# Feed-forward inputs prepared during the attention, and every second tile's gelu turned by a transfer

## The chip, the cores and the metric

The kernel runs on one core of one Trainium2 chip. The metric is the device time in microseconds, as the median of three runs. TensorE (PE) does the matmuls, VectorE (DVE), ScalarE (ACT) and GpSimd (POOL) the work on elements; SyncE (SP) issues nearly all transfers. SBUF is the memory on chip with 128 partitions, PSUM the banks into which TensorE writes, HBM the memory outside.

## The reference

One transformer layer on X of shape (32, 256, 128): `X = X + attention(norm(X))` with 16 heads of size 64, and then `X = X + ffn(norm(X))`. For each token the feed-forward part is

```
h = norm(norm(x)) * g1 + lb1            # 128 numbers
h = gelu(h @ T1 + b1)                   # T1: ternary weights, 128 x 512
h = norm(h) * g2 + lb2                  # 512 numbers
out = h @ T2 + b2                       # T2: ternary weights, 512 x 128
```

There are 8192 tokens, that is 64 tiles of 128 tokens. Nearly float32 precision is wanted, so each operand of a matmul is split in two 16-bit numbers, a high part and the low rest, and a product is three matmuls: high x high, high x low, low x high.

## The kernel before

The program of each engine is written out by hand as a loop over the same steps; semaphores order the engines. `attention_steps` yields pairs (t, u). A step t handles pair t of heads (256 pairs, 8 to a batch of 256 tokens, so t = 8 b + j); from step 80 to 239 two steps are done as one ("paired", `two_steps`). A turn u handles the feed-forward part: in turn u each engine does its piece of tile u minus a lag. Turns 0 to 23 lie beside steps 245 to 268, later turns stand alone. X lies in SBUF throughout, the attention adds its output to it, and `ffn_root` leaves `r1` and `nm1`, the scale and shift of the second norm, for each batch.

Attention, as far as it is touched: TensorE computes queries and keys (`queries_keys`, bank QK), scores for the maxima (`max_scores`, bank M) and scores (bank S, in paired steps also the pair of banks named misc); ScalarE takes the exponentials (`exps`, L1000) and the high halves (QKh L1008, xp L962, O L1023), GpSimd the low halves of p (`p_low`, L1210), of x (`x_low`, L1195) and of the outputs (L1216). `x_norm` (L955) normalises two batches ahead. SP turns x, the shifts and the outputs by transposing transfers.

Feed-forward, tile i of 128 tokens, in four-tile groups g:

- turn i: ScalarE normalises the tile, `f_y` (L1107). After four tiles, y is split (ScalarE and VectorE for the first three groups, then GpSimd: `f_ysplit`, L1292 and L1294), and SP turns the group with one transfer, `turn_y`.
- turn i + 10: TensorE's `f_hidden` (L853 to L855, three matmuls of 512 columns into half of M), ScalarE's gelu into a ring of four f32 tiles a (L1115).
- turn i + 11: TensorE's `f_zT` turns a with four f32 transposes into half of S (L864); ScalarE rounds this to zTh (L1121); VectorE takes the statistics of a (L1600, L1607) and the low part zTl (L1613).
- turn i + 13: TensorE's `f_out`, twelve matmuls (L878 to L880).
- turn i + 14: GpSimd adds the bias to X (L1299). Once per group `f_root` gets the scales (L1281, L1283, L1287).
- turn i + 17: VectorE adds the scaled output to X (L1621), and SP stores four tiles at a time.

gelu's argument is scaled by `s_f1` and the turned copy by `inv_f1`, its reciprocal; the sum is scaled by `s_f12`.

Of the kernel before, what the change touches and what calls it, by code (L numbers as in the profile page):

```python
# [13 lines left out]
P = 128  # L14
# [24 lines left out]
L_BIAS, L_HID, L_ZT, L_OUT, L_SUM = 14, 10, 11, 13, 17  # L39
Y_EARLY = 3  # L40
# [28 lines left out]
    "s_f1", "inv_f1", "s_f12", "T2_less", "bias2"))}  # L69
# [86 lines left out]

def split_groups(b, j):
# [80 lines left out]

def misc_bank_no(kind, key):

    return 0 if kind in ("y", "qk") or kind in ("turn", "spread") and key in ("qk", "pg") else 1
# [8 lines left out]
def layer(nc, x_in, wq_in, wk_in, wv_in, wp_in, bp_in, g1_in, lb1_in, w1_in, b1_in,  # L250
          g2_in, lb2_in, w2_in, b2_in, out):
    with ExitStack() as ctx:
# [26 lines left out]
        inv_f1, s_f12 = sb("inv_f1", [P, 1]), sb("s_f12", [P, 1])  # L279
# [22 lines left out]


# [25 lines left out]
        y = [sb(f"y{i}", [P, FG, D]) for i in range(2)]  # L329
        yp = [sb(f"yp{i}", [P, FG, 2, D], F16) for i in range(2)]  # L330
        yT = [sb(f"yT{i}", [P, FG, 2, P], F16) for i in range(2)]
        a = [sb(f"a{i}", [P, F]) for i in range(A_RING)]
        zTh = [sb(f"zTh{i}", [P, FC, P], F16) for i in range(3)]
        zTl = [sb(f"zTl{i}", [P, FC, P], F16) for i in range(3)]
        st2 = [sb(f"st2_{i}", [P, 6]) for i in range(2)]
# [13 lines left out]
        yt_in = [sem(f"s_ffn_y_transposed{i}") for i in range(2)]  # L349
# [26 lines left out]
        s_zt, s_zhi, s_zlo = (sem(f"s_ffn_{n}") for n in ("zT", "zT_hi", "zT_lo"))  # L376
        s_xb, s_f, s_out = sem("s_ffn_x_plus_bias"), sem("s_ffn_out"), sem("s_ffn_sum")
# [57 lines left out]
        def p_high(r):  # L435

            words = p32[r][:, :, :, :].rearrange("p i m n -> p (i m n)").bitcast(BF16)
            return words.rearrange("p (i m n two) -> p i m n two", i=2, m=NB, two=2)[:, :, :, :, 1]

# [53 lines left out]
        def sp_program(e):  # L493
# [40 lines left out]
            def turn_y(g):  # L534
                e.wait_ge(s_ylo, g + 1)
                if g >= 2:
                    e.wait_ge(s_pre, FG * (g - 1))
                e.dma_start_transpose(yT[g % 2][:, :, :, :].rearrange("p k s n -> p (k s) n"),
                                      yp[g % 2][:, :, :, :].rearrange("p k s d -> p (k s d)")).then_inc(yt_in[g % 2], 16)
# [13 lines left out]
            for t, u in attention_steps():  # L553
# [10 lines left out]
                if u == FG + 1:  # L564
                    turn_y(0)
                if u is not None and u % FG == 0 and FG < u <= NT:
                    turn_y(u // FG - 1)
# [8 lines left out]
        def pe_program(e):  # L576
# [267 lines left out]
            def f_hidden(i):  # L844
                g, k = divmod(i, FG)
                if k == 0:
                    e.wait_ge(yt_in[g % 2], 16 * (g // 2 + 1))
# [9 lines left out]
            def f_zT(i):  # L857
                e.wait_ge(s_a, i + 1)
                if i == 0:
                    e.wait_ge(s_ex, NP)  # L860
                if i >= 2:
                    e.wait_ge(s_zlo, i - 1)
                for c in range(FC):
                    op = e.transpose(z_bank[i % 2][:, c * P:(c + 1) * P], a[i % A_RING][:, c * P:(c + 1) * P], ident[:, :])  # L864
                op.then_inc(s_zt, 1)

            def f_out(i):
                g, k = divmod(i, FG)
                e.wait_ge(s_zlo, i + 1)
                if i == 0:  # L870
                    e.wait_ge(s_qklo, NP)
                elif i == FG:
                    e.wait_ge(s_o, NP)
                elif k == 0:
                    e.wait_ge(s_out, FG * (g - 1))
                o = f_bank(i)[:, k * D:(k + 1) * D]
                for c in range(FC):
                    e.matmul(o, zTh[i % 3][:, c, :], T2h[:, c, :], start=c == 0, stop=False)  # L878
                    e.matmul(o, zTh[i % 3][:, c, :], T2l[:, c, :], start=False, stop=False)
                    op = e.matmul(o, zTl[i % 3][:, c, :], T2h[:, c, :], start=False, stop=c == FC - 1)  # L880
                op.then_inc(s_f, 1)

            def f_out_last(i):
                e.wait_ge(s_zhi, i + 1)
                e.wait_ge(s_x1, B)
                o = last_out
                for c in range(FC):
                    e.matmul(o, zTh[i % 3][:, c, :], T2h[:, c, :], start=c == 0, stop=False)
                    e.matmul(o, zTh[i % 3][:, c, :], T2l[:, c, :], start=False, stop=False)
                e.wait_ge(s_zlo, i + 1)  # L890
                for c in range(FC):
                    op = e.matmul(o, zTl[i % 3][:, c, :], T2h[:, c, :], start=False, stop=c == FC - 1)
# [33 lines left out]
            for t, u in attention_steps():  # L926
# [9 lines left out]
                for lag, fn in ((L_HID, f_hidden), (L_ZT, f_zT)):  # L936
                    if 0 <= u - lag < NT:
                        fn(u - lag)
                if 0 <= u - L_OUT < NT - 1:
                    f_out(u - L_OUT)  # L940
                elif u - L_OUT == NT - 1:
# [4 lines left out]
        def act_program(e):  # L946
# [155 lines left out]
            def f_y(i):  # L1102
                g, k = divmod(i, FG)
                e.wait_ge(s_nm1, i // NB + 1)
                if g >= 2:
                    e.wait_ge(s_ylo, g - 1)
                e.activation(y[g % 2][:, k, 0:D - 1], X[:, i, 0:D - 1], ACT.Identity, scale=r1[:, i:i + 1],  # L1107
                             bias=nm1[:, i:i + 1]).then_inc(s_y1, 1)

            def f_gelu(i):  # L1110
                e.wait_ge(s_pre, i + 1)
                if i >= A_RING:
                    e.wait_ge(s_zt, i - A_RING + 1)
# [3 lines left out]
            def f_zhi(i):  # L1117
                e.wait_ge(s_zt, i + 1)
                if i >= 3:
                    e.wait_ge(s_f, i - 2)  # L1120
                e.activation(zTh[i % 3][:, :, :], z_bank[i % 2][:, :].rearrange("p (c n) -> p c n", c=FC),  # L1121
                             ACT.Identity, scale=inv_f1[:, :]).then_inc(s_zhi, 1)

            def f_yhi(g):
# [611 lines left out]
```

## Time and profile before

| | |
|---|---|
| median of 3 runs | 1002.25 us (1000.64 to 1003.49) |
| span of the profiled execution, first to last instruction | 998.7 us |
| own time of the profiled execution | not listed with the profile; the median stands 3.55 us above the span |
| granted clock of TensorE | 1.00 (full) in all parts |
| busy: TensorE, VectorE, GpSimd, ScalarE | 980.8, 880.0, 837.1, 729.6 us |
| chain of work that ended last | 95% on TensorE |
| transfers | 57.8 MB, mean 58 GB/s |

In a view by lines a row reads: line, engine, operation, output and inputs by their names in the program, shapes, count, then busy time and mean ns of one, then idle time before it. In a timeline the first number is the start, the second the duration, and brackets hold the idle time before, with what ended it. An instruction may start before the end of the one ahead of it on its engine, since their ends overlap; so the distance of two starts tells how long the engine is held. Transposes and matmuls have modelled ends.

### The profile page before, as it was taken

How to read it: one execution, taken by the hardware profiler on the slowest of the kernel's cores; microseconds unless marked ns; L12 is line 12 of the kernel's file. 1: busy time of each engine (PE TensorE's matmuls, PEld its weight loads, DVE VectorE, ACT ScalarE, POOL GpSimd, SP SyncE). 2: the span in 40 equal slices, each digit the busy share in tenths (PEclk: the TensorE clock that was granted, in tenths of full speed). 3: DMA queues.
4: the chain of work that ended last, by engine and by line, in shares of the span. 5: the costliest groups of instructions: out<-in, count | busy, mean ns of one | idle time of the engine just before them, and what ended most of it. 6: DMA issues, size and time to landing. Idle time of an engine off the chain costs nothing.

```text
span 998.7 us, 39391 instructions
## 1 busy us (share of the span) xinstructions
PE 980.8 (98%) x16052; PEld 782.2 (78%) x16052; DVE 880.0 (88%) x1779; ACT 729.6 (73%) x1151; POOL 837.1 (84%) x861
## 2 busy tenths in 40 slices
PE   7899999999999999999999999999999999999998
PEld 6577777778777787887887777888878777788886
DVE  7888988988889888898889988889889988788998
ACT  5687677777767777777777777777777776879995
POOL 6789888989887888888899888888888889866765
PEclk9999999999999999999999999999999999999999
DMA  6112332222331232233222233324222233354343
GB/s 141 38 32 51 53 66 45 43 49 52 74 53 27 51 73 53 52 53 71 55 48 41 48 73 51 53 53 71 46 41 47 52 52 53 69 86 75 77 86 65
DMA packets 203682, 57.82 MB, mean 58 GB/s; under 512 B 185072, under 2 KB 203248, under 8 KB 203504
## 3 DMA queue, kind: packets, MB, share of 16 engines
q1 hardware_dynamic: 201424, 54.79, 29.8%
q8 instruction: 129, 2.11, 0.9%
q10 hardware_dynamic: 2080, 0.52, 0.2%
q14 instruction: 49, 0.40, 0.1%
HBM read 7.21 MB, written 4.19 MB: 11 GB/s over the span
## 4 chain that ended last, share of the span: by engine, by line
PE 95%; DVE 2%; ACT 1%; issue 1%; POOL 1%; DVEq 0%; POOLq 0%; ACTq 0%
PE S L675 11%; PE PV L700 8%; PE M L635 7%; PE PV L702 6%; PE PV L701 6%; PE QK L622 5%; PE QK L623 5%; PE QK L624 5%; PE misc L675 5%; PE S L667 5%; PE S L864 3%; PE M L753 2%; PE M L718 2%; PE M L754 2%; PE M L755 2%; PE misc L667 2%
## 5 line engine op out<-in xcount | busy, mean ns | idle before, releaser
L1210 POOL TENSOR_TENSOR pl<-p 128x1024 f16<-128x1024 f32 x253 | 476.9, 1896 | 39.3 <-ACT p L1000 39.1
L1410 DVE TENSOR_REDUCE negmax<-M 128x4 f32<-128x1024 f32 x252 | 306.8, 1217 | 22.4 <-PE M L635 16.4
L1008 ACT ACTIVATE QKh<-QK 128x512 f16<-128x512 f32 x251 | 149.5, 596 | 155.5 <-PE QK L624 155.3
L1000 ACT ACTIVATE p<-S,s_exp 128x1024 f32<-128x1024 f32 x173 | 192.4, 1112 | 71.8 <-PE S L675 71.2
L700 PEld LDWEIGHTS PV<-V,p 128*128 128x128 bf16 x2048 | 186.8, 98 | 46.4 <-issue 34.5
L700 PE MATMUL PV<-V,p 128*128 128x65 f16 x2048 | 214.9, 194 | 4.0 <-DVE O L1424 2.9
L701 PE MATMUL PV<-V,p 128*128 128x64 f16 x2048 | 213.4, 193 | 0.0
L702 PE MATMUL PV<-V,pl 128*128 128x65 f16 x2048 | 212.6, 194 | 0.0
L1430 DVE TENSOR_TENSOR QKl<-QK,QKh 128x512 f16<-128x512 f32 x251 | 172.4, 687 | 42.2 <-ACT QKh L1008 41.1
L701 PEld LDWEIGHTS PV<-V,p 128*128 128x128 bf16 x2048 | 189.1, 97 | 4.7
L702 PEld LDWEIGHTS PV<-V,pl 128*128 128x128 f16 x2048 | 188.7, 97 | 0.0
L1216 POOL TENSOR_TENSOR O<-O,O 128x512 f16<-128x512 f32 x128 | 148.7, 1162 | 4.1 <-ACT O L1023 3.6
L622 PE MATMUL QK<-xT,Wh 128*128 128x256 f16 x502 | 136.4, 272 | 1.8 <-DVE QKl L1430 1.6
L624 PE MATMUL QK<-xT,Wl 128*128 128x256 f16 x502 | 136.8, 273 | 0.0
L623 PE MATMUL QK<-xT,Wh 128*128 128x256 f16 x502 | 136.6, 272 | 0.0
L1424 DVE TENSOR_TENSOR O<-PV,rsum 128x256 f32<-128x256 f32 x256 | 108.6, 424 | 8.8
L635 PE MATMUL M<-QKh 64*128 64x256 f16 x1016 | 98.5, 271 | 2.3 <-DVE negmax L1410 0.9
L675 PE MATMUL S<-QKh,QKl 64*128 64x256 f16 x692 | 94.5, 269 | 0.0
L675 PE MATMUL S<-QKh 64*128 64x256 f16 x692 | 94.4, 269 | 0.0
L675 PE MATMUL S<-QKl,QKh 64*128 64x256 f16 x692 | 94.4, 269 | 0.0
L1000 ACT ACTIVATE p<-misc,s_exp 128x1024 f32<-128x1024 f32 x80 | 88.7, 1109 | 0.0
L1023 ACT ACTIVATE O<-O 128x512 f16<-128x512 f32 x128 | 79.6, 622 | 0.0
(236 smaller groups left out, 2501.6 us busy)
## 6 DMA issues: line engine op xcount, KB each, us to landing
result<-X SPq DMA_DIRECT2D x15, 256.0 KB, 2.6
X<-in_L_attn_query SPq DMA_DIRECT2D x7, 512.0 KB, 4.8
OT<-O SPq DMA_TRANSPOSE x64, 4.6
shift<-negmax SPq DMA_TRANSPOSE x63, 2.3
O<-in_L_attn_Wk ACTq DMA_DIRECT2D x2, 256.0 KB, 4.3
O<-in_L_attn_Wq SPq DMA_DIRECT2D x2, 256.0 KB, 4.5
O<-in_L_attn_Wv SPq DMA_DIRECT2D x1, 512.0 KB, 3.9
w<-in_L_ffn_w SPq DMA_DIRECT2D x2, 256.0 KB, 5.6
```

Of the source, the lines that this page charges most:

```text
L622: e.matmul(o, Wh[:, i, cols], xh, start=True, stop=False)
L623: e.matmul(o, Wh[:, i, cols], xl, start=False, stop=False)
L624: op = e.matmul(o, Wl[:, i, cols], xh, start=False, stop=True)
L635: op = e.matmul(max_bank(p)[:, i * 512 + t * N:i * 512 + (t + 1) * N], h[rows, 0, t * P:(t + 1) * P], h[rows, 1, :], start=True, stop=True)
L675: op = e.matmul(bank[:, i * 512 + m * N:i * 512 + (m + 1) * N], k[rows, 1, tok], q[rows, 0, :], start=False, stop=n == 2, skip_group_check ...
L700: e.matmul(PV[:, c0:c0 + E + 1], ph[:, i, m, tok], v[:, E:2 * E + 1], start=m == 0, stop=False)
L701: e.matmul(PV[:, c0:c0 + E], ph[:, i, m, tok], v[:, 0:E], start=False, stop=False)
L702: op = e.matmul(PV[:, c0:c0 + E + 1], pl[r][:, i, m, tok], v[:, E:2 * E + 1], start=False, stop=m == NB - 1)
L1000: e.activation(p32[r][:, :, :, :].rearrange("p i m n -> p (i m n)"), score_bank(p)[:, :], ACT.Exp, scale=s_exp[:, :]).then_inc(s_ex, 1)
L1210: e.tensor_tensor(pl[r][:, :, :, :].rearrange("p i m n -> p (i m n)"), p32[r][:, :, :, :].rearrange("p i m n -> p (i m n)"), p_high(r).rea ...
L1410: e.tensor_reduce(dst[:, :, NB * jj:NB * jj + NB], max_bank(p)[:, :].rearrange("p (i t m) -> p i t m", i=2, t=NB), AX.X, ALU.max, negate=T ...
L1430: e.tensor_tensor(QKl[p % QK_RING][:, :, :].rearrange("p i n -> p (i n)"), qk_bank(p)[:, :], QKh[p % QK_RING][:, :, :].rearrange("p i n -> ...
```

## The change

1. y is prepared during the attention. `y_norm` (two normalising activations and a copy on ScalarE) of batch b - 3 stands after step 8 b + 2, `y_low` on GpSimd after 8 b + 4, `turn_y` after 8 b + 6, and `keep_y`, two steps later, writes the turned batch (128 KB) to a buffer in HBM, `y_kept`. The last batches come in turns up to 35. `f_y`, `f_yhi`, `f_ysplit`, `f_ylo` are gone; `load_y` reads a group (256 KB) back in turn 4 g + 6.
2. Tiles 0, 2, ..., 58 (30 tiles) are "in rows". They have no `f_zT`, `f_zhi` or `f_zlo`. ScalarE rounds a to bf16 as it lies (`f_zrow_high`, turn i + 10), GpSimd subtracts (`f_zrow_low`, turn i + 10), and SP turns both halves with one transfer of 256 KB (`turn_z`, turn i + 11). Their `f_out` is in turn i + 15. The other 34 tiles stay as they were, with `f_out` in turn i + 13.
3. zTh is bf16 and not scaled any more; `inv_f1` and `s_f12` are gone, the scale of the sum is `s_f2`. `f_zlo` is a plain subtraction.
4. The bias is added for four tiles at once, sums come in turn i + 18 in place of i + 17.

```
+L_BIAS, L_HID, L_ZT, L_OUT, L_OUT_ROWS, L_SUM = 13, 10, 11, 13, 15, 18
+ROWS_END = NT - 4
+Y_LAG, Y_LOW, Y_TURN, Y_KEEP = 2, 4, 6, 8
+L_LOAD = 6
+def y_batch(t, lag):
+    b, j = divmod(t - lag, HP)
+    return b - 3 if j == 0 and 0 <= b - 3 < B else None
+def in_rows(i):
+    return i % 2 == 0 and i < ROWS_END
...
+            def y_norm(b):
+                e.wait_ge(s_nm1, b + 1)
+                e.wait_ge(s_ylo, b)
+                for t in range(NB):
+                    i = NB * b + t
+                    e.activation(y[:, t, 0:D - 1], X[:, i, 0:D - 1], ACT.Identity, scale=r1[:, i:i + 1],
+                                 bias=nm1[:, i:i + 1]).then_inc(s_y1, 1)
+                e.wait_ge(s_y1, NB * b + NB)
...
+                e.activation(yp[:, :, 0, :], y[:, :, :], ACT.Copy).then_inc(s_yhi, 1)
+            def y_low(b):
+                e.wait_ge(s_yhi, b + 1)
+                e.tensor_tensor(yp[:, :, 1, :], y[:, :, :], yp[:, :, 0, :], ALU.subtract).then_inc(s_ylo, 1)
+            def turn_y(b):
+                e.wait_ge(s_ylo, b + 1)
...
+            def keep_y(b):
+                e.wait_ge(yt_in, 16 * (b + 1))
+                e.dma_start(y_kept[:, b, :], yTb[b % 2][:, :, :, :].rearrange("p t s n -> p (t s n)")).then_inc(y_kept_in, 16)
+            def load_y(g):
+                e.wait_ge(y_kept_in, 16 * (FG // NB * g + FG // NB))
                 if g >= 2:
                     e.wait_ge(s_pre, FG * (g - 1))
...
+            def f_zrow_high(i):
+                n = rows_no(i)
+                e.wait_ge(s_a, i + 1)
+                if n >= 3:
+                    e.wait_ge(zt_in[n % 3], z_turned(n - 3))
+                e.activation(z_rows_high(n), a[i % A_RING][:, :], ACT.Copy).then_inc(s_zrhi, 1)
+            def f_zrow_low(i):
+                n = rows_no(i)
+                e.wait_ge(s_zrhi, n + 1)
+                e.tensor_tensor(z_rows_low(n), a[i % A_RING][:, :], z_rows_high(n), ALU.subtract).then_inc(s_zrlo, 1)
+            def turn_z(i):
+                n = rows_no(i)
+                e.wait_ge(s_zrlo, n + 1)
+                if n >= 3:
+                    e.wait_ge(s_f, OUT_NO[i - 6])
+                e.dma_start_transpose(zT[n % 3][:, :, :, :].rearrange("p s c n -> p (s c) n"),
+                                      zp[n % 3][:, :, :, :].rearrange("p s c n -> p (s c n)")).then_inc(zt_in[n % 3], 16)
...
             def f_out(i):
                 g, k = divmod(i, FG)
...
+                if in_rows(i):
+                    n = rows_no(i)
+                    e.wait_ge(zt_in[n % 3], z_turned(n))
+                    zh, zl = zT[n % 3][:, 0, :, :].bitcast(BF16), zT[n % 3][:, 1, :, :]
+                else:
+                    n = banks_no(i)
+                    e.wait_ge(s_zlo, n + 1)
+                    zh, zl = zTh[n % 3], zTl[n % 3]
...
-                for lag, fn in ((L_HID, f_gelu), (L_ZT, f_zhi), (0, f_y)):
-                    if 0 <= u - lag < NT:
-                        fn(u - lag)
-                if u % FG == FG - 1 and u // FG < Y_EARLY:
-                    f_yhi(u // FG)
+                if 0 <= u - L_HID < NT:
+                    f_gelu(u - L_HID)
+                if 0 <= u - L_ZT < NT and not in_rows(u - L_ZT):
+                    f_zhi(u - L_ZT)
+                if 0 <= u - L_HID < NT and in_rows(u - L_HID):
+                    f_zrow_high(u - L_HID)
```

## Rows read from the trace of the kernel before

**Rows 1.** The page: busy us (share of the span) and instructions of each engine

```profile
PE 980.8 (98%) x16052; PEld 782.2 (78%) x16052; DVE 880.0 (88%) x1779; ACT 729.6 (73%) x1151; POOL 837.1 (84%) x861
```

**Rows 2.** Busy time by stretch: length, engines with counts, granted clock, transfer share, GB/s

```profile
400.00:500.00 100.00, 99.79 (x1762) 80.59 (x1758) 89.22 (x176) 70.80 (x110) 87.91 (x84) 1.00 0.30 58
...
899.00:989.70 90.70, 90.70 (x980) 73.85 (x979) 85.83 (x207) 81.27 (x146) 62.25 (x117) 1.00 0.40 74
```

**Rows 3.** Timeline of a feed-forward turn, 930 to 933 us

```profile
930.51 0.38 PE L853 MATMUL M<-T1h,yT 128*128 128x512 f16 x1
...
930.93 0.23 POOL L1281 TENSOR_SCALAR ve<-mv 128x4 f32<-128x4 f32 x1 [1.37 <-DVE mv L1607]
...
931.16 0.60 PE L864 MATMUL S<-ident,a 128*128 128x128 f32 x4
...
931.36 0.69 ACT L1115 ACTIVATE a<-M,s_f 128x512 f32<-128x512 f32 x1
...
931.59 0.22 PE L878 MATMUL QK<-T2h,zTh 128*128 128x128 f16 x1
...
931.94 0.68 ACT L1121 ACTIVATE zTh<-S,inv_f 128x512 f16<-128x512 f32 x1
...
932.26 0.38 PE L853 MATMUL M<-T1h,yT 128*128 128x512 f16 x1
...
932.38 0.30 POOL L1287 TENSOR_SCALAR rs<-r,s_f 128x4 f32<-128x4 f32 x1
...
932.66 0.75 DVE L1613 SCALAR_TENSOR_TENSOR zTl<-S,inv_f,zTh 128x512 f16<-128x512 f32 x1
```

**Rows 4.** The chain that ended last, 820 us to the end: start, us, what

```profile
873.28 1.75 DVE pl L1442
...
989.21 0.45 PE S L864 x4
```

**Rows 5.** Timeline of VectorE behind the attention, 894 to 897 us

```profile
894.51 0.68 DVE L1600 BATCH_NORM_STATS2 st<-a 128x6 f32<-128x512 f32 x1
...
895.45 0.71 DVE L1613 SCALAR_TENSOR_TENSOR zTl<-S,inv_f,zTh 128x512 f16<-128x512 f32 x1
896.09 0.68 DVE L1600 BATCH_NORM_STATS2 st<-a 128x6 f32<-128x512 f32 x1
```

**Rows 6.** Groups by line, 800 us to the end: GpSimd's subtraction

```profile
L1294 POOL TENSOR_TENSOR yp<-y,yp 128x512 f16<-128x512 f32 x13 | 15.0, 1157 | 1.1
```

**Rows 7.** The yT tile, 900 to 980 us, and busy time in a half microsecond of one

```profile
L538 SPq DMA_TRANSPOSE yT<-yp x12: 1232/1232/1345, 899.7 to 977.0; - x12
...
DMA to landing us min/median/max: 3.1/3.1/4.7
...
943.50:944.00 0.50, 0.50 (x8) 0.49 (x7) 0.50 (x2) 0.39 (x2) 0.10 (x1) 1.00 1.08 208
```

**Rows 8.** Timeline of ScalarE in paired steps, 420 to 427 us

```profile
420.58 1.11 ACT L1000 ACTIVATE p<-S,s_exp 128x1024 f32<-128x1024 f32 x1 [0.63 <-PE S L675]
...
425.52 0.86 ACT L955 ACTIVATE xn<-X,nm,r 128x128 f32<-128x128 f32 x2
426.41 0.42 ACT L962 ACTIVATE xp<-xn 128x256 f16<-128x256 f32 x1
```

**Rows 9.** The chain through the window 400 to 454 us: the next paired scores

```profile
426.27 0.22 PE S L667 x4
```

**Rows 10.** Timeline of GpSimd in the same steps, 420 to 430 us

```profile
420.10 0.22 POOL L1170 TENSOR_SCALAR ve<-mv 128x2 f32<-128x2 f32 x1 [2.49 <-DVE mv L1390]
...
424.64 3.74 POOL L1210 TENSOR_TENSOR pl<-p 128x1024 f16<-128x1024 f32 x2
...
429.46 0.67 POOL L1195 TENSOR_TENSOR xp<-xn,xp 128x256 f16<-128x256 f32 x1
```

**Rows 11.** Timelines of ScalarE and TensorE's weight loads in single steps, 200 to 203 us

```profile
200.40 1.11 ACT L1000 ACTIVATE p<-S,s_exp 128x1024 f32<-128x1024 f32 x1 [0.19 <-PE S L675]
...
202.62 0.11 PEld L667 LDWEIGHTS S<-shift,sel 64*128 64x128 f16 x4 [0.42 <-issue]
```

More of the change, by code:

```diff
@@ L236, in value_order, with rows_no, banks_no, out_turn @@
             yield from two_values(t)
+def in_rows(i):
+    return i % 2 == 0 and i < ROWS_END
+def rows_no(i):
+    return i // 2
+def banks_no(i):
+    return sum(not in_rows(k) for k in range(i))
+def out_turn(i):
+    return i + (L_OUT_ROWS if in_rows(i) else L_OUT)
+OUT_ORDER = sorted(range(NT), key=lambda i: (out_turn(i), i))
+BANKS = [i for i in range(NT) if not in_rows(i)]
+OUT_NO = {i: n + 1 for n, i in enumerate(OUT_ORDER)}
+FIRST_OUT = {min(range(FG * g, FG * g + FG), key=OUT_NO.get): g for g in range(NT // FG)}
+LAST_OUT_NO = {g: max(OUT_NO[i] for i in range(FG * g, FG * g + FG) if i != NT - 1) for g in range(NT // FG)}
+def sums_in(u):
+    last = NT - 2 + L_ZT
+    return [u - L_SUM] if L_SUM <= u < last - 1 else [u - L_SUM, u - L_SUM + 1] if u == last - 1 else []
+def last_sums_in(u):
+    last = NT - 2 + L_ZT
+    return [u - L_SUM] if u > last else []
 def misc_bank_no(kind, key):
@@ L250, in layer @@
 def layer(nc, x_in, wq_in, wk_in, wv_in, wp_in, bp_in, g1_in, lb1_in, w1_in, b1_in,
[L251 removed]
+          g2_in, lb2_in, w2_in, b2_in, y_kept, out):
     with ExitStack() as ctx:
@@ L301, in layer @@
         ve1, r1, mr1, nm1 = (sb(n, [P, NT]) for n in ("ve1", "r1", "mr1", "nm1"))
+        y = sb("y", [P, NB, D])
+        yp = sb("yp", [P, NB, 2, D], F16)
+        yTb = [sb(f"yTb{i}", [P, NB, 2, P], F16) for i in range(2)]
         setup = ExitStack()
@@ L563, in sp_program @@
                         turn_outputs(b, c)
[L564 to L567, printed above, removed]
+                if y_batch(turn_of(t, u), Y_TURN) is not None:
+                    turn_y(y_batch(turn_of(t, u), Y_TURN))
+                if y_batch(turn_of(t, u), Y_KEEP) is not None:
+                    keep_y(y_batch(turn_of(t, u), Y_KEEP))
+                if u is not None and u >= L_LOAD and (u - L_LOAD) % FG == 0 and u - L_LOAD < NT:
+                    load_y((u - L_LOAD) // FG)
+                if u is not None and 0 <= u - L_ZT < NT and in_rows(u - L_ZT):
+                    turn_z(u - L_ZT)
                 if u is not None and 0 <= u - L_SUM < NT - STORE and (u - L_SUM) % STORE == STORE - 1:
@@ L935, in pe_program @@
                     e.wait_ge(s_lo, LO_AT["T2l"])
-                for lag, fn in ((L_HID, f_hidden), (L_ZT, f_zT)):
-                    if 0 <= u - lag < NT:
-                        fn(u - lag)
-                if 0 <= u - L_OUT < NT - 1:
-                    f_out(u - L_OUT)
-                elif u - L_OUT == NT - 1:
+                if 0 <= u - L_HID < NT:
+                    f_hidden(u - L_HID)
+                if 0 <= u - L_ZT < NT and not in_rows(u - L_ZT):
+                    f_zT(u - L_ZT)
+                for i in OUT_ORDER:
+                    if out_turn(i) == u and i < NT - 1:
+                        f_out(i)
+                if u == out_turn(NT - 1):
                     f_out_last(NT - 1)
@@ L1672, in dve_program @@
                     continue
-                if u == 0:
-                    for i in range(2):
-                        e.memset(y[i][:, :, D - 1:D], 1.0).then_inc(s_y0, 1)
-                if u % FG == 0 and 0 < u // FG <= Y_EARLY:
-                    f_ylo(u // FG - 1)
                 tiles = {NT - 2: (NT - 2, NT - 1), NT - 1: ()}.get(u - L_ZT, (u - L_ZT,) if 0 <= u - L_ZT < NT else ())
```

186 lines of the change are left out of this document (90 added, 96 removed).

## The prediction

> **What bounds the kernel now.** The page's busy times come first: TensorE is busy 98% of the span, more than VectorE, GpSimd or ScalarE [rows 1]. A share over the span hides stages, so the busy time by stretches is next. In the attention (400 to 500 us) TensorE is busy 99.79 of 100 us, GpSimd 87.9, VectorE 89.2, ScalarE 70.8; in the pure feed-forward stage (899 to 989.7 us) TensorE is busy all of 90.7 us, VectorE 85.8, ScalarE 81.3, GpSimd 62.3 [rows 2]. TensorE's clock is at its full level in both. Matmul ends are modelled, so a busy engine can still wait for up to some 0.2 us unseen; the timeline of one turn settles it [rows 3]. A turn runs from one L853 to the next: 932.26 - 930.51 = 1.75 us. In it the three hidden matmuls take 931.16 - 930.51 = 0.65 us, the four f32 transposes 931.59 - 931.16 = 0.43 us, the twelve output matmuls 932.26 - 931.59 = 0.67 us, with nothing between. The chain of waits agrees: after VectorE's p_low at 873 us and the few pieces behind it, it goes through TensorE alone to 989 us, and the transposes stand on it turn after turn with 0.44 or 0.45 us; the last such row is at 989.21 [rows 4]. So what TensorE no longer does in that stage comes off the end, as long as no other engine takes over at once.
>
> How far are the others? VectorE looks nearly full, but part of that is waiting for the high half: zTl starts at 932.66, just as zTh (931.94 + 0.68) ends [rows 3]. Right after the attention, when VectorE has a backlog, it does a tile in 896.09 - 894.51 = 1.58 us [rows 5]. That is its real limit.
>
> **Part 1: the transposes of 30 tiles.** Even tiles below 60 lose f_zT: 30 x 0.43 = 12.9 us off TensorE (by the chain's 0.44, 13.2). Their hidden and output matmuls stay as many and as wide. Odd tiles and the last four keep all. Hence turns alternate, 1.75 and 1.75 - 0.43 = 1.32 us, a pair 3.07 us.
>
> The others per pair. VectorE: one zTl less, and in the backlog it holds the engine for 896.09 - 895.45 = 0.64 us [rows 5]: 2 x 1.58 - 0.64 = 2.52 us, below 3.07. ScalarE: gelu holds it for 931.94 - 931.36 = 0.58 us, zTh (as long an instruction) for as much, and the normalising L1107 is gone; the high half in rows is of the size of zTh: 4 x 0.58 = 2.3 us, below 3.07. GpSimd per four tiles: two subtractions in rows, like L1294 of the same size, 2 x 1.16; the bias of four tiles in one instruction of 128x512, by the same row 1.2 [rows 6]; the roots 932.38 + 0.30 - 930.93 = 1.75 [rows 3]. Together 5.3 us in 6.14, so 86%. It fits, and it is the tightest.
>
> **Part 2: does the turned tile arrive in time?** This trace has no transfer of z, but the yT transfer has its size (256 KB) and form. From the start of hidden(i) at T: gelu starts at T + 0.85 and ends at T + 1.54 (931.36 in a turn that began at 930.51, + 0.69) [rows 3]. zTh of the tile before runs from T + 1.43; the high half in rows starts some 0.57 later and ends near T + 2.65; GpSimd's low half ends near T + 3.9 (1.16, and small semaphore delays). SP spends 1.23 us on such an issue, and from issue to landing it is 3.1 us, at most 4.7 [rows 7]: T + 7.0, at worst T + 8.6. f_out of a row tile is five turns later, behind that turn's hidden: 3 x 1.75 + 2 x 1.32 + 0.65 = 8.54. The slack is 1.5 us at the median and nothing at the worst. Taken: no wait in the steady stage, and 0.5 us in all in the first tiles, where z shares the queue with the last attention outputs (512 KB each). Bounds: nothing, and 6 us (rival 1).
>
> Is there room on the transfer engines? A turning transfer goes at 208 GB/s while the engines' share is 1.08, so that is their full pace: 262144 B / 208 GB/s = 1.26 us [rows 7]. Per four tiles (6.14 us) there will be two z transfers, one store and one load of y_kept, 256 KB each. The two plain ones have no row of their own here; at the turning pace it is 4 x 1.26 = 5.0 of 6.14 us. On SP's queue the same four tiles take four issues, 4.9 us even at 1.23 each. load_y sits between a store and the next turn_z and waits for hidden matmuls of the turn before, which are done by then; the store that precedes it waits for a sum one turn earlier. So nothing behind them, above all turn_z, is held long.
>
> The Trainium skill (VectorE: DVE Perf Modes, "The three transpose paths" and "Rules for kernel authors") speaks against such a move: TensorE for a 128x128 transpose if PSUM will do, 390 ns there against 1309 ns by the transfer. Taken as eight blocks one behind the other that is an estimate of 10.5 us for a z tile, more than the lead, and the gain would be lost; the row of yT, eight blocks landed in 3.1 us together, contradicts the sum but not the rule's order of the two latencies.
>
> The Trainium skill (DMA: Bandwidth & Descriptors, "Latency and other measured facts") gives 261 GB/s for a transposing transfer; the trace's 208 is lower, and by 261 a z tile would land 0.25 us sooner, with the same sum.
>
> **Part 3: y prepared in the attention.** Per batch ScalarE gets two y_norm activations and a copy. x_norm and x_high are of the same shapes: 0.86 us for two and 0.42: 1.28 us [rows 8]. In the paired steps (20 batches) it stands after the last QKh of a step with j = 2. ScalarE is idle for 0.63 us before the exponential at 420.58 [rows 8], so that one comes 1.28 - 0.63 = 0.65 us late and ends at 422.3. TensorE wants its bank S again at 426.27 [rows 9], GpSimd reads it from 424.64 on [rows 10]: nothing. GpSimd's y_low is like x_low, 0.67 us, put behind x_low at 429.46; the next paired subtraction starts later by that, and the 2.49 us in which GpSimd waits for VectorE's statistics before 420.10, once per batch, swallow it [rows 10]. The low halves in between are read by TensorE only in the next paired step, behind its scores: nothing again, and at most the 0.67 us a batch if that slack is gone.
>
> In the single steps (7 batches, and those near the end) ScalarE has 0.19 us free before the exponential at 200.40. It will start at 201.49 and end at 202.60, where TensorE's next scores, which need the bank, start at 202.62 [rows 11]: 0 to 0.1 us a batch. Taken for the attention: 0.6 us; bounds 0 and, if every delay reached TensorE, 20 x 0.65 + 8 x 1.1 = 22 us (rival 2). The new transfers there (128 KB turned and 128 KB written per batch) stand on SP behind the turned outputs, and the next shift comes at least two steps after them: nothing.
>
> **Part 4: the changeover and the small edits.** The early turns lose ScalarE's L1107 and VectorE's subtraction of y, and get one y_norm in eight. The chain passes VectorE at 873 us [rows 4], so a little comes back; taken -0.4 us, bounds 0 and -1.5. A plain subtraction in place of zTl's three-operand form, a copy in place of the scaled one, two fewer weight scalars, the y fill at the start (before VectorE waits for x) and the sums one turn later: nothing, because TensorE covers them; uncovered, the first would give back some hundredths of a us a tile. The end, two tiles on VectorE, the last outputs and eight sums, stays.
>
> **Sum.** -12.9 + 0.5 + 0.6 - 0.4 = -12.2 us. The profiled span is 998.7, so the new span is 986.5. The profile lists no time of its own for that execution; the median of the three runs shown is 1002.25, 3.55 more. With the same distance: 990.0 us.
>
> **Rivals.**
> 1. *z lands late.* For: the worst landing in the trace uses up all the slack, and there will be twice as many turning transfers and a load beside them. Against: issues 3 us apart, engines at 82% by the slower pace. If landings lie 0.5 us past the slack, each five turns stretch by that: 60 / 5 x 0.5 = 6 us, so 996. At 1.1 us too late the gain is gone. 992 to 1000. Chance 18%.
> 2. *Slower: y_norm on the path of the exponentials.* Place: between the last QKh of a j = 2 step and the next exponential. From 12.2 / 32 = 0.4 us a batch on it eats the gain; in full, 22 us, the time is 1012. For: ScalarE's delay of 0.65 to 1.1 us is sure. Against: the slack behind it, above. Chance 7%.
> 3. *Another engine takes over the feed-forward turns.* GpSimd at 86% in a strict order is the candidate; at 3.5 us a pair, that is 7 us per four tiles, nothing is won: 1002. It would need 1.7 us more than the rows give. Chance 5%.
> 4. *More comes back at the changeover*, and the transposes count 0.44: 988. It shares the first case's range.
>
> The forecast (TensorE stays the bound, 987.5 to 993) has 70%. About 0.3% (3 us) can be told from no change. Faster takes the forecast, nearly all of rival 1 and half a percent of the others: 88%; same 5%; slower 7%. The range for 8 in 10 is 987 to 998: the forecast's own and rival 1 but its end.
>
> **What would show it.** Right: no L864 in odd turns, outputs following hidden matmuls directly, pairs of 3.07 us, TensorE without gaps from 880 us on, batches of the attention as long as before. Rival 1: TensorE or its weight load waiting for a transfer ahead of f_out, landings over 4 us. Rival 2: a longer batch, scores waiting for ScalarE. Rival 3: turn_z issued ever later behind GpSimd.

## The result, and the profile after

The kernel with the change takes 995.47 us (median of four runs, 993.86 to 996.55), the kernel before 1002.25 (median of three, 1000.64 to 1003.49; a fourth execution, of 1397.82 us, is left out) in the same comparison; the ratio is 0.9937 with a 95% interval of 0.9926 to 0.9949. A repetition gave 996.48 against 1001.68, ratio 0.9943 (0.993 to 0.9955). So the change gains 5.7 to 6.3 us, about half of the 12.2 that were forecast. The direction was right, 995.5 lies in the range of 987 to 998, and the size is wrong. The profiled execution is the fastest of the four: its span is 992.1 us and its own time 993.86, so 1.76 us lie around the span.

The page after, busy us of each engine (share of the span) and instructions, beside [rows 1]:

```profile
PE 969.8 (98%) x15932; PEld 768.5 (77%) x15932; DVE 854.8 (86%) x1743; ACT 732.8 (74%) x1180; POOL 861.5 (87%) x849
```

TensorE has 120 instructions fewer (30 tiles of four transposes) and is still busy 98% of the span. Busy time by stretch after, with the columns of [rows 2]:

```profile
400.00:500.00 100.00, 99.77 (x1757) 80.31 (x1755) 89.23 (x175) 74.55 (x121) 91.25 (x86) 1.00 0.34 68
899.00:983.00 84.00, 82.23 (x902) 63.15 (x898) 66.73 (x183) 62.12 (x106) 68.23 (x84) 1.00 0.82 165
```

The attention looks as it did: ScalarE and GpSimd carry 3 to 4 us more in 100, TensorE is as full as before. In the feed-forward stage TensorE is no longer busy all the time: 82.23 of 84.00 us, where before it was 90.70 of 90.70. VectorE and ScalarE have plenty of room (66.7 and 62.1 of 84), and the transfer engines' share has gone from 0.40 to 0.82. The timeline of TensorE, one pair of turns:

```profile
908.73 0.38 PE L943 MATMUL M<-T1h,yT 128*128 128x512 f16 x1
...
909.38 0.22 PE L977 MATMUL PV<-T2h,zT 128*128 128x128 f16 x1
...
910.05 0.38 PE L943 MATMUL M<-T1h,yT 128*128 128x512 f16 x1
...
910.70 0.60 PE L955 MATMUL S<-ident,a 128*128 128x128 f32 x4
...
911.13 0.22 PE L977 MATMUL PV<-T2h,zTh 128*128 128x128 f16 x1
```

In the turn of a tile in rows the outputs follow the hidden matmuls at once: 910.05 - 908.73 = 1.32 us. The next turn keeps its transposes (911.13 - 910.70 = 0.43) and takes 1.75. A pair is 3.07 us, as forecast. The gain is lost elsewhere. The waits of 890 to 985 us (engine, line, waited for: us, times, longest) say where:

```profile
PEld M L943 <- DMA yT<-y_kept: 2.9, 7, 0.7
PE M L943 <- DMA yT<-y_kept: 1.6, 4, 0.6
```

TensorE waits for the load of y for a group of four tiles. The weight load and the matmul behind it share some of these waits, so I read the sum from the turns (the turn of tile i lasts from its hidden matmuls to those of tile i + 1): at the starts of tiles 8, 20, 28, 32, 40, 44, 52 and 60 the turn before is longer than 1.32 us by 0.25, 0.31, 0.18, 0.53, 0.16, 0.14, 0.66 and 0.73, together 3.0 us. The chain through one of them, start, us, what:

```profile
923.21 0.22 PE M L943
...
924.96 0.64 ACT zp L1241
...
925.67 1.17 POOL zp L1407
926.85 1.23 SPq L624
928.14 1.56 SPq L630
929.80 3.14 DMA yT<-y_kept
932.98 0.39 PE M L943
```

This is the loss in seven lines. The hidden matmuls of tile 26 (923.21) give the gelu whose low half GpSimd writes at 925.67. SP stands at the turning transfer of that tile (L624) until 926.84, issues it for 1.23 us, then issues a store of results (L630), and only then the load of y (L616), whose data lands 3.14 us later, at 932.94. TensorE wanted it at 932.45. The load itself waits for nothing late: it stands behind an issue that does.

From the first hidden matmuls (873.96) to the last (983.00) it is 109.04 us, where before it was 117.63 (872.52 to 990.15): 8.6 us less. The transposes of 30 tiles are 13.1 us. Outside of this stretch the first hidden matmuls start 1.44 us later, and the end behind the last takes 9.10 instead of 8.55 us. 8.59 - 1.44 - 0.55 = 6.6 = 998.7 - 992.1.

The longer end is no loss, but work that moved. The outputs of tile 58 now come two turns later, in the last turn with hidden matmuls, together with those of tile 60:

```profile
983.64 0.60 PE L955 MATMUL S<-ident,a 128*128 128x128 f32 x4
984.08 0.22 PE L977 MATMUL QK<-T2h,zT 128*128 128x128 f16 x1
...
984.75 0.22 PE L977 MATMUL PV<-T2h,zTh 128*128 128x128 f16 x1
...
985.42 0.60 PE L955 MATMUL S<-ident,a 128*128 128x128 f32 x4
```

That is 0.67 us more in this turn; and 0.67 us of outputs are missing from the turn of tile 3 (1.32 us, before 2.42), because those of tile 0 moved out of it. So of the 8.6 us only 7.9 are transposes that came off.

### The profile page after: what moved, and what is told of

It is laid out like the page before. It is cut to its first block, busy times and chain, and to the rows that moved or that the text cites. A ratio compares the mean times of both kernels' runs of the same rounds, so it can differ in the third digit from the quotient of the medians.

```text
span 992.1 us, 39212 instructions
## 1 busy us (share of the span) xinstructions
PE 969.8 (98%) x15932; PEld 768.5 (77%) x15932; DVE 854.8 (86%) x1743; ACT 732.8 (74%) x1180; POOL 861.5 (87%) x849
## 4 chain that ended last, share of the span: by engine, by line
PE 90%; DVE 2%; ACT 2%; DMA 2%; issue 2%; SPq 1%; POOL 1%; DVEq 0%; ACTq 0%
PE S L765 11%; PE PV L790 8%; PE M L725 7%; PE PV L792 6%; PE PV L791 6%; PE QK L713 5%; PE QK L712 5%; PE QK L714 5%; PE misc L765 5%; PE S L757 5%; PE M L843 2%; PE M L808 2%; PE M L844 2%; PE M L845 2%; PE misc L757 2%; PE M L810 2%
```

## The experiments

There are sixteen runs; a0, e4_again and b0 repeat a kernel. "Before" is the kernel before, run in the same comparison; ratios are to it. e2, e7 and b0 to b3 are one execution each, so they have no ratio.

**a0_again: the change as it is, again.**

> The changed kernel as it is, beside its variants. The profile of the change shows pairs of turns of 3.07 us, as forecast, but TensorE late at the first tile of many groups of four (0.14 to 0.73 us each, some 3 us in all), where it waits for the load of y, and 1.2 us lost in the first 20 us of the kernel. Theory A (the load of y is issued too late, because it stands on SP's queue behind a turning transfer and a store): the same waits at the same tiles, ratio 0.993 to 0.995. Theory B (the 1.2 us at the start are an accident of one execution, not of the change): the first reductions of the weights end near 8.3 us as before, the span is up to 1.2 us shorter. If B falls they end near 9.2 us again.

996.48 us, ratio 0.9943 (0.993 to 0.9955). The waits at the groups' first tiles are there again, at other tiles and in other sizes (1.25 us at tile 52, 0.67 at 44); in all they are 4.6 us in this profile, of an execution of 996.48 us, where the profile of 993.86 us had 3.0. So Theory A holds, but for the tiles and sizes. Theory B, that the late start is an accident, falls: the first loads run at 236 GB/s again, where the kernel before has 288 (see b0 to b3).

**e1_load5: the load of y one turn earlier.**

```
-L_LOAD = 6
+L_LOAD = 5
```

> The load of y for each group issued one turn earlier, which puts it ahead of that turn's turning transfer and store on SP. Theory A: the load is issued some 3 us earlier relative to its group, the waits of TensorE at the first tile of a group vanish, and the time is 2.5 to 3.5 us less than that of the unchanged variant. Rival R (the waits come from the transfer engines being full, share 0.86, or from turned tiles): the waits stay or move to the turned tiles, and the time moves by less than 1 us.

991.95 us (990.77 to 992.52), ratio 0.9899 (0.9884 to 0.9914), against 0.9943 for the change beside it: 4.5 us gained by one constant. That is more than the 2.5 to 3.5 expected, which came from the 3.0 us of one profile, and just what a0's 4.6 us of waits would give. SP's queue in this kernel:

```profile
924.53 1.23 SPq L624 DMA_TRANSPOSE zT<-zp  x1
926.44 0.33 SPq L616 DMA_DIRECT2D yT<-y_kept  x1
927.60 1.23 SPq L624 DMA_TRANSPOSE zT<-zp  x1
928.89 1.39 SPq L630 DMA_DIRECT2D result<-X  x1
```

The load now stands ahead of a transfer of z, not behind it and the store, and is issued at 926.44 for hidden matmuls at 933.01. No wait for yT is left in the stage; every group starts after 1.32 us. The traffic is the same as in the change, so full transfer engines (Rival R) weren't the cause. The largest waits of TensorE that remain there:

```profile
PEld S L955 <- ACT a L1226: 1.0, 1, 1.0
...
PE S L955 <- ACT a L1226: 0.5, 1, 0.5
```

**e2_load8: the opposite dose, the load two turns later than in the change.**

```
-L_LOAD = 6
+L_LOAD = 8
```

> The change with the load of y for a group of four tiles put two turns later still (turn 4g+8 instead of 4g+6, where e1 had 4g+5). Theory A (the load is issued behind the turning transfer of z, which waits for GpSimd, about 6.0 us after the start of the turn two before it, and lands 3.3 us later, so 9.4 us; the group's first hidden matmuls come four turns, 6.14 us, after the same start): TensorE waits 2.4 to 3.3 us at the first tile of each of 15 groups, span 1020 to 1045 us. Rival (these waits have another cause than the load's place in SP's queue): within 3 us of the change, 993 to 999.

1027.91 us (one execution), span 1026.1: in the expected range, and the span 34 us longer than the change's. The waits for the load of y, 890 to 985 us:

```profile
PE M L943 <- DMA yT<-y_kept: 20.0, 10, 5.7
PEld M L943 <- DMA yT<-y_kept: 15.8, 9, 3.8
```

From 984 us on each group's first tile comes 1.8 to 2.1 us late (turns of 3.15 to 3.38 us for 1.32), a little less than expected. Earlier ones are longer, and one of them shows a second cost (last section).

**e4_load5_ynorm_last and e4_again: e1, and y_norm behind the gelu and the rounding in the feed-forward turns.**

```
-                if y_batch(turn_of(t, u), Y_LAG) is not None:
-                    y_norm(y_batch(turn_of(t, u), Y_LAG))
                 if u is None:
+                    if y_batch(t, Y_LAG) is not None:
+                        y_norm(y_batch(t, Y_LAG))
                     continue
...
                 if 0 <= u - L_HID < NT and in_rows(u - L_HID):
                     f_zrow_high(u - L_HID)
+                if y_batch(turn_of(t, u), Y_LAG) is not None:
+                    y_norm(y_batch(turn_of(t, u), Y_LAG))
```

> As the variant with the earlier load, and in the late steps that share turns with the feed-forward part the normalising of y stands behind ScalarE's gelu and rounding instead of ahead of them. Theory: in the profile of the change the turns of batches 29 and 31 hold up gelu by 1.3 us, and TensorE loses some 0.9 and 0.4 us there, so 1.0 to 1.3 us less than with the earlier load alone. Rival: TensorE's loss there is from something else (banks, the last attention outputs), then within 0.3 us of it.

> The version with the load one turn earlier and y_norm last, unchanged, beside the one above on the same chip: 991.1 (990.3 to 991.9).

991.09 us, ratio 0.9895 (0.9881 to 0.9908), and again 990.39, ratio 0.9889 (0.9871 to 0.9906). Beside e1 that is 0.4 us by the ratios of the same comparison and 1.0 by the repetition's, less than expected. In the change y_norm of a late batch holds ScalarE ahead of a gelu:

```profile
911.96 0.63 ACT L1241 ACTIVATE zp<-a 128x512 bf16<-128x512 f32 x1
912.48 0.87 ACT L1209 ACTIVATE y<-X,nm,r 128x127 f32<-128x127 f32 x2
913.38 0.42 ACT L1216 ACTIVATE yp<-y 128x256 f16<-128x256 f32 x1
913.70 1.28 ACT L1226 ACTIVATE a<-M,s_f 128x512 f32<-128x512 f32 x2
```

The turn of tile 20 takes 2.16 us there (2.47 in e1) and 1.76 in e4: that came back. At the other place, the turns of tiles 4 and 5, TensorE stopped waiting for the gelu and waited for the first turned z instead (2.42 and 3.10 us in e4 for 3.59 and 1.99 in e1), so nothing came back there.

**e3_norows: no tile in rows, the rest of the change kept.**

```
-ROWS_END = NT - 4
+ROWS_END = 0
```

> The change without tiles in rows: y is prepared in the attention, kept in HBM and loaded, and all 64 tiles are turned by TensorE. Forecast by the steps of the prediction: no gain in the feed-forward turns (1.75 us each), the attention 0.4 us longer (that is what the profile of the change shows behind the first 20 us), so 0 to 1.5 us slower than before. Rival (preparing y early costs or gains by itself, a few us): outside of that.

1013.87 us, ratio 1.0121 (1.0107 to 1.0135): the expectation missed. The sums were left one turn later (18) while the outputs, with no tile in rows, came at 13 turns as before; a bank of outputs was freed in the very turn in which it was wanted, and every fourth turn took 2.65 us:

```profile
PE PV L977 <- DVE X L1730: 4.2, 5, 1.2
```

**e3b_norows_sum17: the same with the sums where the kernel before has them.**

```
-... L_OUT_ROWS, L_SUM = ... 15, 18
-ROWS_END = NT - 4
+... L_OUT_ROWS, L_SUM = ... 15, 17
+ROWS_END = 0
```

> Only the preparation of y in the attention, its way through HBM and the bias by fours; all tiles turned by TensorE, and the sums at their old lag of 17 turns. With the lag of 18 this variant took 1013.9 us, because each group's first output matmul waited for the sum that frees its bank (one turn of 2.65 us in four). Theory: that wait is gone, turns are 1.75 us throughout, and what is left is the start (1.0 to 1.3 us) and 0.3 us in the attention, less some at the changeover: 1001 to 1004 us. Rival: the load of y or the attention costs more by itself: above 1005.

1002.71 us (eleven runs), ratio 1.0009 (1.0 to 1.0017). Turns are 1.75 us from tile 11 on, and it is 117.53 us from the first hidden matmuls to the last. So all of the change but the rows (preparing and keeping y, the bias by fours, the simpler rounding) costs 0 to 1.7 us, at the median 0.9, when it brings nothing. e5 below, which is e4 but for the place of a buffer, ran in the same comparison and took 991.3 us: 11.4 us less. That is about what the rows are worth when nothing waits for the load.

**e6_more_scalar: e4, and one more activation of the normalising's shape in each feed-forward turn (its output is used by nothing).**

```
                 if 0 <= u - L_HID < NT:
                     f_gelu(u - L_HID)
+                    more_scalar(u - L_HID)   # 128x127, Identity with scale and bias
```

> The best version so far (load one turn earlier, y_norm behind the gelu) plus one more activation of 128x127 per feed-forward turn on ScalarE, of the shape of the normalising that the change moved to the attention; its output is used by nothing. Theory: ScalarE then has 2 x 0.58 (gelu) + 2 x 0.58 (high halves) + 2 x 0.49 = 3.3 us a pair of turns with nothing between, more than TensorE's 3.07, and becomes the bound: pairs of 3.3 us, 30 x 0.23 = 7 us lost, 998 (995 to 1001). Rival: ScalarE overlaps enough, TensorE stays the bound and moving the preparation of y to the attention was not needed: 991 to 993.

994.55 us, ratio 0.9925 (0.9908 to 0.9941): 3 us lost, neither the 7 of the theory nor the 0 to 2 of the rival. ScalarE's timeline, one pair of turns:

```profile
970.76 0.69 ACT L1233 ACTIVATE a<-M,s_f 128x512 f32<-128x512 f32 x1
971.35 0.48 ACT L1222 ACTIVATE y_more<-ident,nm,r 128x127 f32<-128x127 f32 x1
971.74 0.58 ACT L1240 ACTIVATE zTh<-S 128x512 bf16<-128x512 f32 x1
972.21 0.62 ACT L1248 ACTIVATE zp<-a 128x512 bf16<-128x512 f32 x1
972.73 0.68 ACT L1233 ACTIVATE a<-M,s_f 128x512 f32<-128x512 f32 x1
973.30 0.49 ACT L1222 ACTIVATE y_more<-ident,nm,r 128x127 f32<-128x127 f32 x1
973.84 0.69 ACT L1233 ACTIVATE a<-M,s_f 128x512 f32<-128x512 f32 x1
```

Instructions overlap at their ends: the starts are 0.59, 0.39, 0.47, 0.52, 0.57 and 0.54 us apart, 3.08 for the pair, just TensorE's 3.07. ScalarE is full without a gap, and keeps up. What costs the 3 us are isolated waits of TensorE: for a gelu in the turns of tiles 14 and 22 (2.50 and 2.70 us for 1.75), for a turned z in those of tiles 29 and 43 (2.58 and 1.88 us for 1.32). So ScalarE does not become the bound of every pair, but leaving the normalising in the stage would have cost some 3 of the 10.6 us; what the dummy lacks is the copy to halves and GpSimd's part.

**e7_rows_out13: e4 with two turns less between the hidden matmuls of a tile in rows and its outputs.**

```
-L_OUT_ROWS = 15
+L_OUT_ROWS = 13
```

> The best version so far with the output matmuls of row tiles three turns behind their hidden matmuls instead of five (two turns, 3.07 us, less lead for the transfer). By the slack read before (z ready 7.0 us after its hidden matmuls, needed after 8.54) they would be wanted 5.5 us after: TensorE waits 1.5 us for each row tile that isn't already delayed, at best every fourth turn: 15 to 30 waits, +23 to +45 us, span 1010 to 1035. If the transfer has much more slack than read: under 995.

1024.69 us (one execution), span 1022.8: in the expected range, but not by z alone. TensorE waits for z, 890 to 985 us:

```profile
PEld QK L977 <- DMA zT<-zp: 12.7, 8, 2.4
PEld PV L977 <- DMA zT<-zp: 12.3, 10, 2.3
```

Beside them stand waits of another kind, for a sum of VectorE:

```profile
959.09 0.22 PE L977 MATMUL QK<-T2h,zT 128*128 128x128 f16 x1 [1.18 <-DMA zT<-zp]
967.23 0.22 PE L977 MATMUL PV<-T2h,zT 128*128 128x128 f16 x1 [1.18 <-DVE X L1732]
```

This is the wait of e3: with outputs at 13 turns and sums at 18, a group's bank is freed in the very turn in which it is wanted. Between 915 and 1009 us the bank is what TensorE waits for at the first tile of seven groups, 1.18 us each, 8.3 us together; so the 34 us or so against e4 are not the price of z alone, and e7 tests two things at once. What it does show is when z is there. At the twelve waits behind 890 us that z ended, the outputs start 6.9 to 9.8 us after the tile's hidden matmuls, four of them at 6.9 to 7.0 and ten within 8.4 (959.09 above is tile 32, whose hidden matmuls began at 952.07: 7.02). So the 7.0 us of the prediction are the best case, at least in e7 with its stretched turns; a slack of 1.5 us holds for such a tile, and others have next to none.

**The start: b0_before_again, b1_before_buffer, b2_before_moved, b3_before_fill, e5_buffer_first.** The first hidden matmuls come 1.44 us later in the change, and most of that is there after the first 20 us. b0 is the kernel before; b1 adds the buffer y_kept in HBM with one small write near the end; b2 puts three unused tensors of the sizes of y, yp and yTb where the change has them; b3 adds the small fill at 1.6 us; e5 is e4 with y_kept declared ahead of the inputs.

> The kernel before, unchanged, for a second profile of its start. All four profiles of variants of the change load the first weights and X at some 218 GB/s between 4 and 6 us, the one profile of before at 288 GB/s, and the first maxima of scores start at 14.1 us there, at 15.1 to 16.2 us in the variants. Theory S (the start belongs to the change): 288 GB/s and 14.1 us again. Rival (chance of the execution): 218 GB/s and 15 us or more.

> The kernel before with the buffer of the change in HBM, into which one transfer of constants writes near the end (about 2 us on the last stores, nothing else uses it). Theory S1 (the buffer's place in HBM shifts the other tensors and slows the first loads): loads at 218 GB/s and the first maxima at 15 us or later. Rival S2 (the start is slowed by something else of the change, its SBUF tensors or its program): 288 GB/s and 14.1 us as before.

> The kernel before with three SBUF tensors of the sizes of y, yp and yTb declared, unused, ahead of the temporaries of the start, so that these and all later tensors lie at other addresses, as in the change. If the addresses set the pace of the first loads: about 218 GB/s between 3.5 and 6 us and first maxima of scores near 14.8 us or later, as in the kernels with the change. If not: 288 GB/s and 14.1 to 15.3 us, as in the three profiles of the kernel before.

> The kernel before with one more small fill on VectorE at 1.6 us, at the place where the change fills y. It is the one instruction that the change adds within the first 5 us. If it (or what it shifts) slows the first loads: about 218 GB/s between 3.5 and 6 us. If not: 288 GB/s; then neither HBM tensor, nor addresses, nor this fill is the cause, and it stays open.

> As the variant with the earlier load and the later y_norm, but the HBM buffer declared ahead of the inputs. Theory S1: the inputs come to lie elsewhere; if place matters the first loads change their rate, to 288 GB/s at best, and 1.0 to 1.3 us come back. Rival S2: 218 GB/s and the same time within 0.5 us.

b0 to b3 gave 1002.87, 1002.89, 1001.09 and 1001.70 us, e5 991.3 (ratio 0.9895, 0.988 to 0.991), as e4. Busy time from 3.5 to 6 us in b2, and then in the change; the last column is GB/s:

```profile
3.50:6.00 2.50, 2.50 (x13) 2.50 (x13) 1.25 (x6) 0.00 (x0) 2.26 (x4) 1.00 1.28 288
```

```profile
3.50:6.00 2.50, 2.50 (x16) 2.28 (x14) 0.41 (x3) 0.00 (x0) 2.26 (x4) 1.00 1.32 233
```

The others of each kind agree: 286 to 289 GB/s in all five profiles with the old code, 233 to 237 in all thirteen of kernels made from the change, e3b and e5 among them (218 once the rate has settled, from 4.2 us on). Where the clock is at its full level, VectorE's first maxima of the scores then start at 14.79 to 15.13 instead of 14.07 to 14.10 us. So 0.7 to 1.0 us at the start belongs to the change; neither the buffer, nor its place, nor the addresses in SBUF, nor the fill is the cause. It stays open.

**e8_z_first and e9_load_z_first: e4 with the transfer of z at the head of SP's step, alone (e8) or with the load of y ahead of it (e9).**

```
             for t, u in attention_steps():
+                if ...: load_y((u - L_LOAD) // FG)        # e9 only
+                if ...: turn_z(u - L_ZT)
                 if t is not None:
                     ...                                   # turn_outputs, turn_y, keep_y as before
```

> The best version so far, with the turning transfer of z put at the head of SP's step, ahead of the transfer of the last attention outputs and of keep_y, wherever both fall into one turn. Theory: z of tile 0 is ready for its transfer at 880.3 us but was issued at 883.7, because SP stood at the transfer of attention outputs, whose data came at 881.4; issued at once it lands in time, the 1.4 us for which TensorE waited for it in the turn of the sixth hidden matmuls go, and with it 1.0 us (0.5 to 1.5) of the whole: 990.1. Rival: the attention outputs, now behind z, come later by as much and the final projection takes the wait: no change, 991.

> As the last one, but with the load of y at the head of SP's step too, ahead of the turning transfer of z. In the last run the place named behaved as the theory said (the turn of the sixth hidden matmuls 1.99 instead of 3.10 us), while in the turns that have both the load of y had come to stand behind the transfer of z, and TensorE waited for the load again, once per group of four tiles. Theory (a load of y loses its time by the transfer of z that it stands behind, in whatever turn): the waits for the load go again and 1.0 us remains gained against the version with the load one turn earlier and y_norm last: 990.1 (989 to 991). Rival (the head of SP's step itself costs, because the turned attention outputs come later): 993 to 995.

e8 is worse, 994.61 us, ratio 0.9929 (0.9916 to 0.9943), though the turn of tile 5 fell from 3.10 to 1.99 us as expected. With the transfer at the head, the load of y stood behind it again, and the waits of the change were back:

```profile
PEld M L943 <- DMA yT<-y_kept: 4.8, 4, 1.9
PE M L943 <- DMA yT<-y_kept: 4.1, 4, 1.8
```

e9 puts only that right, and they are gone: 990.51 us, ratio 0.9897 (0.9879 to 0.9915), 3 us better than e8 by the ratios. But beside e4 (990.39 on the same chip) nothing is gained. The early z transfers that I moved ahead delay the last attention outputs (SP takes up their transfer at 883.87 us, in e4 at 881.45), and a later z waits in turn: the profiled e9 has turns of 1.77 and 3.12 us before tiles 8 and 10, where e4 has 1.32. That profile is of the slowest of its five executions, 993.59 us; three took 990.0 to 990.5, and no profile shows whether they have these waits. In none of them is the expected 1.0 us against e4 to be seen.

The best kernel is e4: its medians lie 10.6 and 10.7 us below those of the kernel before beside it, where the change's lie 5.2 to 6.8 below.

## Why the prediction was half right

1. *TensorE bounds the stage; 30 x 0.43 us come off.* Right in kind and size where nothing else intervenes: pairs of 3.07 us in the change, and with the loads mended (e4) 105.3 to 105.6 us from first to last hidden matmuls, 12 us less than the 117.6 of before; 0.67 of these 12 are the outputs of tile 0 that moved.

2. *The other engines per pair.* Right as bounds. ScalarE needs less than the 2.3 us I summed, since e6 fits two more activations of 0.5 us into 3.08. GpSimd holds its order (rival 3 fell): bias of four tiles 1.27 us (1.2 taken), low half in rows 1.16, as taken.

3. *z arrives at T + 7.0 with a slack of 1.5.* Right for the best tiles, a little bold for the others. Landings have a median of 3.5 us (3.1 taken), at most 4.5; in the change TensorE's weight load waited for z once, 0.5 us, but in other profiles TensorE waited for that of tile 24, 0.29 us in a0, 1.10 in e6 and 0.91 in e9, where the outputs start 9.2 to 9.8 us after the tile's hidden matmuls. So the bound "at worst T + 8.6" was too low. Rival 1 gave nearly the measured time, 996, but by another mechanism: that the time lies in the stated range is luck. In e4 the rows are worth 10.6 us against before, 11.4 against e3b, on the engine that bounds; the turned tile lands 3.6 us after its issue at the median, and apart from the first tile (0.94 us) no turn of e4 is longer than it should be by more than 0.13 us. The Trainium skill (VectorE: DVE Perf Modes, "The three transpose paths") ranks TensorE ahead of the transfer for 128x128 by latency; the ranking holds here too (0.11 us each on TensorE, against 3.5 us for eight in one transfer), and it does not decide, since the transfer's latency is hidden and TensorE's time is not.

4. *"So nothing behind them, above all turn_z, is held long", and with it "Taken: no wait in the steady stage".* This is the step that failed. I asked what load_y and the store would hold up, and never what holds up load_y, nor when its data is needed: the wait for the load was put at nothing without a sum. By my own numbers: the turn_z ahead of the load turns tile i and is issued at T + 3.9, with T the start of the hidden matmuls of tile i; its issue takes 1.23 us, a store ahead of the load about 0.6 (0.57 at the median here, at most 1.56), the landing 3.1: T + 8.8. The group's hidden matmuls come six turns, three pairs, later: T + 9.2. That is a slack of 0.4 us, where z has 1.5, and a landing of 3.3 to 4.1 or a store issue of 1.56 uses it up. In the chain above it was T + 9.7 (932.94 - 923.21). What the runs showed in its place: 3.0 us of waits for the load in the profile of the change, 4.6 in a0's. That the load's place is the cause is shown by three doses: one turn earlier, no wait and 4.5 us gained; two turns later, 1.8 to 2.1 us a group in the steady part and 32 us lost; one place back in the queue (e8), the waits return, and e9 takes them away again.

5. *Preparing y in the attention costs 0.6 us.* Right in size: 0.9 with bounds 0 and 1.7 (e3b), but most of it is likely the slower first loads (0.7 to 1.0 us), which no term had. The attention behind them adds less than the 0.6: ScalarE's exponentials near 50 us start 1.24 us later than before (50.78 for 49.54), the first hidden matmuls 1.44, so 0.2 us. Rival 2 fell. What the term lacked is its end: the last batches are normalised in feed-forward turns, ahead of a gelu, for 0.4 to 0.7 us at tile 20. I had written "one y_norm in eight" and costed the work, not its place in the order.

6. *The changeover gives 0.4 us back.* Wrong sign: the early turns lose 1.8 of the 13.1 us. The turns of tiles 4 and 5 take 3.59 and 2.21 us, where 2.42 and 1.99 would be due (2.42 before, less the transposes in the second), because ScalarE prepares y there and SP stands at the last attention outputs when z of tile 0 is ready. And the transposes of tile 0 brought nothing: TensorE waits longer for VectorE in that turn instead, which takes 4.06 us after 4.04. "The end stays" is wrong by the 0.67 us that moved into it, without a loss. e4 and e9 each moved the wait elsewhere without a measurable gain at this place.

7. *The distance of 3.55 us from span to time.* It is 1.75 to 1.93 us in every execution of kernels made from the change, and 1.8 to 2.4 in those of the kernel before (b0: 1002.87 for a span of 1001.0; b2: 1001.09 for 998.7). Executions of the kernel before with a span of 998.7 to 998.9 us took 1000.51 to 1001.19. So the profiled one was a fast one, not one with a long way around it, and the 3.55 us mixed it with slower ones; the predicted gain is unchanged by that.

In numbers: -12.2 forecast, -6.6 in the span of the profile. Of the 13.1 us of the transposes, waits for the load of y took 3.0 (4.5 by e1's ratio), y_norm ahead of the gelu of tile 20 0.4, the early turns 1.8, the start 1.2, the attention 0.2: 6.6, where 13.1 - 6.6 = 6.5 is to be explained. All are read from one profile of each kernel. Of the start's 1.2 us, 0.7 to 1.0 have no known cause; the rest goes with the lower clock that this profile has there (last section).

## What to carry to other kernels

When a transfer is put into an in-order queue, work out three things for it and not one: when its data is ready, when each instruction ahead of it will have been issued (a transfer that waits for an engine holds everything behind it, ready or not), and when its result is needed. The dangerous one is not the new, tight transfer that everybody looks at, but the easy one next to it. And when a large saving leaves the bound engine nearly full, list its waits by what they wait for before anything else: one row gave the cause, and one constant gave 4.5 us.

## What the runs showed of the hardware

A wait can cost more than its length. In e2, behind a wait of 3.4 us, TensorE's granted clock stood at 0.50, its lower level of 1.2 GHz, for the next turn:

```profile
962.28 0.50 PE L943 MATMUL M<-T1h,yT 128*128 128x512 f16 x1 [3.42 <-DMA yT<-y_kept]
```

```profile
957.00:962.00 5.00, 1.85 (x25) 1.32 (x22) 2.82 (x9) 1.85 (x4) 3.32 (x4) 1.00 0.87 135
962.50:965.50 3.00, 3.00 (x19) 2.40 (x18) 0.35 (x1) 1.67 (x3) 0.00 (x0) 0.50 0.33 91
```

The engine was busy 1.85 us of the 5.00 from 957 us on; then four transposes took 0.87 us for 0.44 and the turn 3.28 for 1.75. In the first 20 us the clock is lower too in 9 of 13 profiles of the kernels made from the change and in one of five of the kernel before (0.83 or 0.91 over that stretch). The first maxima then start at 15.25 us in the kernel before (14.1 at full level) and at 15.31 to 17.04 in the others (14.79 to 15.13). But the lower level doesn't belong to the change: 24 of the 49 executions of the kernel before in these comparisons have a mean clock of 0.997 or 0.998 and a span of 999.7 to 1001.1 us, the other 25 one of 998.7 to 998.9. So a comparison of two single profiles can be off by 1 to 2 us from this alone.

The turning transfers of z lost little beside twice the traffic: with the transfer engines' share at 0.82 they landed in 3.1 to 4.5 us, at the median 3.5 (the turned y before: 3.1 at a share of 0.40); the plain load of the same 256 KB took 2.9 to 4.1, at the median 3.3. So a plain load lands hardly sooner than a turning one of this size; what it spares is the issue, 0.49 us at the median (0.33 in e1) against 1.23.
